# Pairs and layer-1 blocks two to a PSUM bank, one stage order for another, and the first ids spread by TensorE

## The chip, the cores and the metric

The kernel runs on one core of a Trainium2 chip. The metric is the device time of one execution in microseconds (us). The engines are TensorE (PE in the rows; PEld is its weight load), VectorE (DVE), ScalarE (ACT), GpSimd (POOL) and SyncE (SP), which here only issues DMAs.

## The reference: what is computed

A recommender tower for 2048 samples. Per sample 26 ids pick one row of 128 floats from each of 26 tables; with the dense row these are 27 features. All pairwise dot products go with the dense row into three layers.

```python
e = jnp.stack([tbl_0[ids[:, 0]], ..., tbl_25[ids[:, 25]]], axis=1)       # 2048 x 26 x 128
combined = jnp.concatenate([dense[:, None, :], e], axis=1)               # 27 features
inter = jnp.einsum('bfd,bgd->bfg', combined, combined)[:, TRIU_I, TRIU_J]  # 351 pairs
h = jnp.concatenate([dense, inter, dense], axis=1)
h = jnp.maximum(h @ W_top1 + b_top1, 0.0)        # 607 -> 512
h = jnp.maximum(h @ W_top2 + b_top2, 0.0)        # 512 -> 256
y = h @ W_top3                                   # 256 -> 1
```

## The kernel before

The batch is cut into 8 steps of 256 samples (`NB`, `BS`), two tiles of 128 each. The rows of a sample come in two ways.

- Ten small tables (1000 rows) are held in SBUF as two parts, `table_hi` and `table_lo`. A **lookup** is a multiplication by a one-hot matrix: ACT writes the spread ids into PSUM (`idb`, L555), DVE compares them with the row numbers in two chunks (L651, three slots `SLOTS`), PE multiplies 16 times (L411, L412). In step 0 four of the tables are taken from the raw table instead (L409). The ids arrive spread over 128 partitions by one DMA for each lookup (L275), the first ten of them into free places of `rows`.
- The other 16 tables are **gathered** from HBM by indirect DMAs of GpSimd (L359), 128 rows each, in groups of eight. After the first five, group g waits until products stage g-4 is done (`wait_for_turn`), so each products stage lets one burst of eight gathers go. PE transposes what landed (`rows`, L431), ACT or DVE copies it into `XT` (L567, L666).

The **products** of a step are four stages of 64 small products (L449: one record for each half, 128 records), copied by ACT and DVE in turn (L573, L659). **Unblock** (L461, copies L578 and L674) and **pairs** (L472, copies L584) bring the products into the layout that **layer1** (L483, L485; four blocks), **layer2** (L494; two blocks) and **layer3** (L503) take; their results leave by ACT (L588, L595).

The order of all this is one list written out by hand, `stages()`, and PE, ACT, DVE and SP each walk through it and do their part. Layers run one step behind the products, lookups one step ahead. All stages but the products share a ring of four PSUM banks in the order of the list: before PE fills a bank it waits until the bank's last user but three has been copied out (`claim`). So whoever waits for a copy, waits for everything that stands before it on ACT or DVE.

In what follows a step has four **quarters**, each from the end of one products stage to the end of the next; the first begins behind products 0.

## Time and profile before

| | us |
|---|---|
| median of 3 runs (lowest, highest) | 520.28 (514.35, 523.56) |
| the profiled execution | 515.3 |
| its span, first to last instruction | 513.2 |
| granted TensorE clock, mean | 0.88 |
| busy: PE, DVE, POOL, ACT | 408.8, 262.7, 254.1, 208.7 |
| chain that ended last: PE, issue, ACT, SPq, DMA | 71%, 13%, 4%, 4%, 4% |

All positions in time are those of the profiled execution, whose own time lies 2.1 us over its span. A granted clock of 1.00 is 2.4 GHz and one of 0.50 is 1.2 GHz; values between are means over a stretch.

### The profile page before, as it was taken

The numbers are of one execution on the slowest core, as the hardware profiler recorded it, in microseconds if no ns is written. First come the engines' busy times: TensorE is split into PE (matmuls) and PEld (weight loads), VectorE is DVE, ScalarE is ACT, GpSimd is POOL, SyncE is SP. The second block draws the span as 40 slices with busy tenths as digits, with TensorE's granted clock in tenths as the row PEclk, the third lists the DMA queues.
The fourth block names the chain that finished last, engine by engine and source line by source line (L and its number), as shares of the span: only waits on it lengthen the run. The fifth ranks groups of instructions, "written<-read, shape, count | busy, mean of one in ns | idle before, by whom it ended". The sixth has DMA issues, their size and how long they took to land.

```text
span 513.2 us, 14192 instructions
## 1 busy us (share of the span) xinstructions
PE 408.8 (80%) x6280; PEld 365.9 (71%) x6280; DVE 262.7 (51%) x323; ACT 208.7 (41%) x436; POOL 254.1 (50%) x265
## 2 busy tenths in 40 slices
PE   5886727777978598875978788887989689789977
PEld 4776716767878497764967687785878588778755
DVE  3789505654555554663553655655364655454220
ACT  3456302234343543444342553435243543337432
POOL 5778875551555555552555535553555535540000
PEclk8998857776999898988897978997898969899989
DMA  6994251230322222221222212221232212210000
GB/s 170 227 240 107 67 158 50 70 108 23 74 59 78 56 64 68 69 64 32 64 66 70 63 49 64 67 74 49 68 68 69 63 42 70 58 39 1 4 1 0
DMA packets 27972, 36.34 MB, mean 71 GB/s; under 512 B 9151, under 2 KB 21959, under 8 KB 27912
## 3 DMA queue, kind: packets, MB, share of 16 engines
q1 hardware_dynamic: 19704, 18.65, 14.6%
q0 software_dynamic: 8192, 16.79, 13.5%
q8 instruction: 49, 0.80, 0.6%
q14 instruction: 11, 0.09, 0.0%
q10 hardware_dynamic: 16, 0.01, 0.0%
HBM read 35.42 MB, written 0.01 MB: 69 GB/s over the span
## 4 chain that ended last, share of the span: by engine, by line
PE 71%; issue 13%; ACT 4%; SPq 4%; DMA 4%; DVE 2%; another core or an unknown queue 1%; ACTq 0%; DVEq 0%
PE ring L411 17%; PE ring L412 15%; PE gram L449 10%; PE ring L485 8%; PE ring L431 7%; PE ring L494 6%; DMA dense<-in_r_dense_features 4%; PE ring L483 3%; SPq L281 2%; PE ring L461 2%; PE ring L472 2%; DVE pairs_and_more L674 2%; PE ring L503 2%; ACT pairs_and_more L578 1%; SPq L275 1%
## 5 line engine op out<-in xcount | busy, mean ns | idle before, releaser
L359 POOL DMA_INDIRECT rows<-in_tbl,ids_all x256 | 248.7, 971 | 201.1 <-PE gram L449 127.3
L651 DVE TENSOR_TENSOR onehot<-idb,vrow 125x1024 fp32r<-125x1024 f32 x160 | 192.7, 1222 | 130.5 <-PE ring L412 58.7
L411 PE MATMUL ring<-onehot,table_hi 125*128 125x256 f32 x608 | 181.6, 328 | 22.1 <-DVE pairs_and_more L674 7.6
L412 PE MATMUL ring<-onehot,table_lo 125*128 125x256 f32 x608 | 169.5, 309 | 0.0
L411 PEld LDWEIGHTS ring<-onehot,table_hi 125*128 125x128 f32 x608 | 132.9, 219 | 28.8 <-issue 8.7
L412 PEld LDWEIGHTS ring<-onehot,table_lo 125*128 125x128 f32 x608 | 133.4, 219 | 0.8
L559 ACT COPY xt<-ring 128x256 f32<-128x256 f32 x80 | 54.2, 677 | 128.9 <-PE ring L412 68.3
L449 PE MATMUL gram<-xt 128*27 128x26 f32 x4096 | 55.1, 201 | 42.6 <-issue 40.0
L449 PEld LDWEIGHTS gram<-xt 128*27 128x27 f32 x4096 | 47.8, 114 | 51.7 <-issue 46.0
L567 ACT COPY xt<-ring 128x512 f32<-128x512 f32 (+1 forms) x56 | 51.2, 987 | 24.1 <-remote 16.0
L431 PE MATMUL ring<-ident,rows 128*128 128x128 f32 x256 | 38.6, 285 | 13.6 <-issue 6.7
L485 PE MATMUL ring<-x,w 128*128 128x256 f32 (+1 forms) x192 | 47.7, 385 | 0.0
L666 DVE COPY xt<-ring 128x512 f32<-128x512 f32 x24 | 28.4, 1183 | 31.5 <-PE ring L431 19.7
L431 PEld LDWEIGHTS ring<-ident,rows 128*128 128x128 f32 x256 | 30.8, 147 | 18.2 <-issue 10.0
L485 PEld LDWEIGHTS ring<-x,w 128*128 128x128 f32 (+1 forms) x192 | 37.5, 195 | 5.6
L588 ACT ACTIVATE h<-ring,b 128x256 f32<-128x256 f32 x32 | 15.2, 475 | 55.8 <-PE ring L485 17.8
L659 DVE COPY A<-gram 128x416 f32<-128x416 f32 x16 | 14.2, 886 | 42.3 <-PE gram L449 42.3
L674 DVE COPY pairs_and_more<-ring 64x80 f32<-64x80 f32 (+6 forms) x112 | 22.1, 197 | 22.3 <-PE ring L431 12.6
L494 PE MATMUL ring<-h,w 128*128 128x256 f32 x128 | 31.5, 391 | 1.0 <-ACT h L588 1.0
L555 ACT CAST idb<-ids_spread 128x256 f32<-128x256 int32 x70 | 30.6, 437 | 3.6 <-ACT pairs_and_more L595 2.0
L494 PEld LDWEIGHTS ring<-h,w 128*128 128x128 f32 x128 | 24.0, 196 | 4.7 <-ACT h L588 1.8
L578 ACT COPY pairs_and_more<-ring 64x104 f32<-64x104 f32 (+5 forms) x96 | 21.2, 221 | 10.7 <-PE ring L431 9.4
(41 smaller groups left out, 209.7 us busy)
## 6 DMA issues: line engine op xcount, KB each, us to landing
ids_spread<-in_ids_t SPq DMA_DIRECT2D x70, 128.0 KB
rows<-in_tbl,ids_all POOLq DMA_INDIRECT x256
xt<-in_tbl SPq DMA_DIRECT2D x6, 448.0 KB
w<-in_tbl SPq DMA_DIRECT2D x3, 448.0 KB
rows<-in_ids_t SPq DMA_DIRECT2D x10, 128.0 KB, 5.7
dense<-in_r_dense_features SPq DMA_DIRECT2D x16, 64.0 KB
w<-in_W_top SPq DMA_DIRECT2D x4, 256.0 KB
w<-in_W_top SPq DMA_DIRECT2D x1, 512.0 KB
```

Of the source, the lines that this page charges most:

```text
L359: pool.indirect_dma_start(rows[:, i % ROWS, :], None, aps[f"tbl_{f}"], bass.IndirectOffsetOnAxis(ap=ids_all[:, k, f:f + 1].bitcast(U32), a ...
L411: pe.matmul(ps, table_hi[:, m, c * KC + k, :], chosen, start=first, stop=False)
L412: last = pe.matmul(ps, table_lo[:, m, c * KC + k, :], chosen, start=False, stop=final)
L431: last = pe.transpose(ps[:, i * P:(i + 1) * P], src, ident[:])
L449: last = pe.matmul(gram[QW * j:QW * j + F, s % 2, g * NA:(g + 1) * NA], sample, sample[:, 0:NA], start=True, stop=True)
L485: last = pe.matmul(ps, w1[0:w, 1 + k, b * P:(b + 1) * P], x[0:w, k, :], start=False, stop=(k == KX - 1))
L494: last = pe.matmul(ps[:, 0:BS], w2[:, k, b * P:(b + 1) * P], h1[:, k, :], start=(k == 0), stop=(k == H1 // P - 1))
L555: act.copy(idb[:, u % 2, 0:BS], ids_place(u)).then_inc(idb_ready, 1)
L559: act.copy(XT[:, n % 2, :, 1 + NG + m], ps[:, 0:BS]).then_inc(left("lookup", n, m, 0), 1)
L567: act.copy(rows_view(n, t, g), ps[:, 0:f * P].rearrange("d (f s) -> d f s", f=f)).then_inc(left("rows", n, t, g), 1)
L651: dve.tensor_tensor(onehot[:, (CH * u + c) % SLOTS], idb[0:VP, u % 2, 0:BS].unsqueeze(1).to_broadcast([VP, KC, BS]), vrow[:, c * KC:(c + 1 ...
L674: last = dve.tensor_copy(dst, src)
```

## The change

- The pairs take two ring banks instead of three, layer1 two instead of four: two blocks of 256 columns lie side by side in a bank. ACT copies the first two pair blocks with one instruction, and still does one activation for each layer-1 block, but PE is told of the bank only after both.
- `stages()` is another list: in a steady step some other work stands between any two lookups; pairs go from the end of a step to the first quarter of the next; layer1 is two stages instead of four; rows 0 and 1 of the next step move from the last quarter to the third; layer3 moves to the end of the last quarter.
- ACT now copies all of tile 0's rows and products 1 and 3; DVE copies rows 1 and 3 of tile 1 and products 0 and 2.
- The ids of the first ten lookups come as one small DMA of ten rows. ACT turns them into floats, and PE spreads each over the partitions with one multiplication (`spread_first_ids`); the ten broadcast DMAs, and GpSimd's waits for their places, are gone. `ids_all`, which the gathers need, is issued after that small DMA. The dense tiles are loaded between the tables instead of after them.
- DVE makes the first chunk of a lookup one stage earlier, and `lower_part` before the chunks.

```diff
-        yield from lookups(0, *range(NL - 2))
-        yield from rows(0, 0, 0, 1)
-        yield from lookups(0, NL - 2)
-        yield from rows(0, 0, 2, 3, 4)
+        yield "first_ids", 0, 0, 0
+        yield "first_ids", 0, 1, 0
+        for m in range(NL - 1):
+            yield from lookups(0, m)
+            if m + 2 < NL:
+                yield "first_ids", 0, m + 2, 0
+        yield from rows(0, 0, 0, 1, 2, 3, 4)
         yield from lookups(0, NL - 1)
         for n in range(NB):
+            first, last = n == 0, n == NB - 1
             yield "products", n, 0, 0
             yield from lookups(n + 1, 0)
+            yield from layer("pairs", n - 1, 0, 1)
+            yield from lookups(n + 1, 1)
             yield from layer("layer1", n - 1, 0)
-            yield from lookups(n + 1, 1)
-            yield from layer("layer1", n - 1, 1)
+
+            yield "products", n, 1, 0
             yield from lookups(n + 1, 2)
-
-            yield "products", n, 1, 0
-            if n == 0:
+            if first:
                 yield from lookups(n + 1, 3)
             yield from rows(n, 1, 0, 1)
-            yield from layer("layer1", n - 1, 2)
-            if n > 0:
+            yield from layer("layer1", n - 1, 1)
+            yield from rows(n, 1, 2, 3, 4)
+            if not first:
                 yield from lookups(n + 1, 3)
-            yield from rows(n, 1, 2, 3)
-            yield from layer("layer1", n - 1, 3)
-            yield from rows(n, 1, 4)
+            if last:
+                yield from layer("layer2", n - 1, 0)
+
+            yield "products", n, 2, 0
             yield from lookups(n + 1, 4)
-            if n == NB - 1:
+            if not last:
                 yield from layer("layer2", n - 1, 0)
-
-            yield "products", n, 2, 0
             yield from lookups(n + 1, 5)
-            if n < NB - 1:
-                yield from layer("layer2", n - 1, 0)
+            yield from rows(n + 1, 0, 0, 1)
+            if not last:
+                yield from layer("layer2", n - 1, 1)
             yield from lookups(n + 1, 6)
-            yield from layer("layer2", n - 1, 1)
+
+            yield "products", n, 3, 0
+            if last:
+                yield from layer("layer2", n - 1, 1)
             yield from lookups(n + 1, 7)
-            if n < NB - 1:
-                yield from layer("layer3", n - 1, 0)
-
-            yield "products", n, 3, 0
-            if n == NB - 1:
-                yield from layer("layer3", n - 1, 0)
+            yield from layer("unblock", n, 0, 1)
             yield from lookups(n + 1, 8)
-            yield from layer("unblock", n, 0, 1)
-            yield from rows(n + 1, 0, 0, 1)
             yield from layer("unblock", n, 2, 3)
             yield from rows(n + 1, 0, 2, 3, 4)
             yield from lookups(n + 1, 9)
-            yield from layer("pairs", n, 0, 1, 2)
-        yield from layer("layer1", NB - 1, 0, 1, 2, 3)
+            yield from layer("layer3", n - 1, 0)
+        yield from layer("pairs", NB - 1, 0, 1)
+        yield from layer("layer1", NB - 1, 0, 1)
...
+            sp.dma_start(first_ids_i, aps["ids_t"][:, 0:BS]).then_inc(first_ids_landed, 16)
             sp.dma_start(ids_all[:], ids.rearrange("(t p) f -> p t f", p=P)).then_inc(ids_landed, 16)
             for m in range(NL):
-                spread_ids(m)
                 load_raw(m)
-            load_dense(0)
-            load_dense(1)
+                if m in (3, 6):
+                    load_dense(m // 4)
...
+            def spread_first_ids(m):
+                if m == 0:
+                    pe.wait_ge(first_ids_ready, 1)
+                if m >= 2:
+                    pe.wait_ge(onehot_ready, CH * (m - 1))
+                pe.matmul(idb[0:VP, m % 2, 0:BS], ident[0:NL, m:m + 1].to_broadcast([NL, VP]), first_ids, start=True,
+                          stop=True).then_inc(first_idb_ready, 1)
...
+                bank = claim("layer1", n, b, 0)
+                for i in range(2):
+                    ps, block = bank[:, i * BS:(i + 1) * BS], slice((2 * b + i) * P, (2 * b + i + 1) * P)
+                    pe.matmul(ps, w1[:, 0, block], x_dense[:, n % 2, :], start=True, stop=False)
+                    if b == i == 0:
+                        wait_emptied("pairs", n, 1, 0)
```

On PE, the second quarter of a steady step, behind its first lookup; the names are those of the stages above (`dense` and `rows` are row transposes, `x_dense` and `x` layer1). Before, it begins with products 1:

```order
L449 MATMUL gram<-xt 27x26 x64
L431 MATMUL ring<-ident,dense 128x128
L431 MATMUL ring<-ident,rows 128x128 x7
L483 MATMUL ring<-x_dense,w 128x256
L485 MATMUL ring<-x,w 128x256 x3
L411 MATMUL ring<-onehot,table_hi 128x256
L412 MATMUL ring<-onehot,table_lo 128x256
```

After the change, from the last multiplication of that quarter's first lookup to the first of its second:

```order
L418 MATMUL ring<-onehot,table_lo 128x256
L437 MATMUL ring<-ident,dense 128x128
L437 MATMUL ring<-ident,rows 128x128 x7
L490 MATMUL ring<-x_dense,w 128x256
L495 MATMUL ring<-x,w 128x256 x3
L490 MATMUL ring<-x_dense,w 128x256
L495 MATMUL ring<-x,w 128x256 x3
L437 MATMUL ring<-ident,rows 128x128 x9
L417 MATMUL ring<-onehot,table_hi 128x256
```

Two layer-1 blocks and all the remaining row transposes now stand in one piece ahead of the lookup, where one block stood before.

On PE, the last quarter of a steady step, before: both halves of unblock (`A`), with rows 0 and 1 of the next step between them.

```order
L461 MATMUL ring<-ident,A 128x128 x6
L431 MATMUL ring<-ident,dense 128x128
L431 MATMUL ring<-ident,rows 128x128 x7
L461 MATMUL ring<-ident,A 128x128 x7
L431 MATMUL ring<-ident,rows 128x128 x9
L411 MATMUL ring<-onehot,table_hi 128x256
```

After the change, the same place from the last multiplication of the lookup that now stands between the halves:

```order
L418 MATMUL ring<-onehot,table_lo 128x256
L467 MATMUL ring<-ident,A 128x128 x7
L437 MATMUL ring<-ident,rows 128x128 x9
L417 MATMUL ring<-onehot,table_hi 128x256
```

A lookup has taken the place of rows 0 and 1; what stands behind it, the second half of unblock, nine transposes and a lookup, is unchanged.

On ACT, the end of that quarter after the change, from the row copies to the next step's first pairs:

```order
L574 COPY xt<-ring 128x4x128 x2
L574 COPY xt<-ring 128x128
L562 CAST idb<-ids_spread 128x256
L566 COPY xt<-ring 128x256
L610 COPY pairs_and_more<-ring 1x4x64
L615 DMA out_y<-pairs_and_more 1x256
L562 CAST idb<-ids_spread 128x256
L566 COPY xt<-ring 128x256
L591 COPY x<-ring 128x512
L591 COPY x<-ring 95x256
```

Before, three copies L584 of the pairs stand directly behind the first L559 there, and the output copy two lookups further up.

## Rows read from the trace of the kernel before

**Rows 1.** Windows: us; busy PE, PEld, DVE, ACT, POOL; clock; DMA share; GB/s.

```profile
303.20:316.30 13.10, 11.58 (x194) 10.59 (x193) 6.03 (x5) 4.74 (x9) 7.56 (x8) 0.96 0.28 70
316.30:330.20 13.90, 12.02 (x195) 11.01 (x194) 7.94 (x8) 5.57 (x10) 7.57 (x8) 0.92 0.25 57
330.20:343.10 12.90, 11.53 (x197) 10.43 (x197) 6.83 (x6) 5.10 (x10) 7.57 (x8) 1.00 0.29 79
343.10:360.50 17.40, 13.50 (x203) 11.81 (x203) 10.66 (x22) 9.32 (x25) 7.56 (x8) 0.78 0.22 54
460.40:471.80 11.40, 10.27 (x203) 9.21 (x203) 6.78 (x18) 8.22 (x22) 0.00 (x0) 1.00 0.02 4
...
126.40:446.30 319.90, 264.87 (x4301) 241.21 (x4301) 172.81 (x208) 133.50 (x285) 166.47 (x176) 0.90 0.26 63
...
387.50:401.80 14.30, 12.89 (x198) 11.79 (x199) 6.43 (x7) 5.37 (x11) 7.56 (x8) 0.90 0.29 71
105.90:126.20 20.30, 15.43 (x204) 13.92 (x203) 10.78 (x21) 9.01 (x23) 7.56 (x8) 0.67 0.16 44
```

**Rows 2.** Timeline, POOL: start, us, instruction, idle before, its releaser.

```profile
303.49 0.95 POOL L359 DMA_INDIRECT rows<-in_tbl,ids_all  x1 [7.11 <-PE gram L449]
...
312.26 0.94 POOL L359 DMA_INDIRECT rows<-in_tbl,ids_all  x1 [0.30 <-issue]
```

**Rows 3.** Timeline, PE: the products stage behind the burst of rows 2.

```profile
312.54 0.37 PE L449 MATMUL gram<-xt 128*27 128x26 f32 x14
...
314.84 1.49 PE L449 MATMUL gram<-xt 128*27 128x26 f32 x111 [0.54 <-issue]
```

**Rows 4.** Timeline, PE and ACT: layer2's second block and its activation.

```profile
335.77 1.89 PE L494 MATMUL ring<-h,w 128*128 128x256 f32 x8
...
340.42 0.47 ACT L588 ACTIVATE x<-ring,b 128x256 f32<-128x256 f32 x1 [2.89 <-PE ring L412]
```

**Rows 5.** Timeline, all engines: the last quarter of step 4.

```profile
343.02 0.38 PE L411 MATMUL ring<-onehot,table_hi 125*128 125x256 f32 x1
...
343.38 0.94 POOL L359 DMA_INDIRECT rows<-in_tbl,ids_all  x1 [3.21 <-PE gram L449]
...
345.04 0.82 PE L461 MATMUL ring<-ident,A 128*128 128x128 f32 x6
...
347.28 1.02 PE L461 MATMUL ring<-ident,A 128*128 128x128 f32 x7 [0.29 <-issue]
...
351.88 1.49 DVE L674 COPY pairs_and_more<-ring 64x32 f32<-64x32 f32 x8 [2.38 <-remote]
353.43 0.58 PE L411 MATMUL ring<-onehot,table_hi 125*128 125x256 f32 x1 [1.35 <-issue]
354.75 2.45 ACT L567 COPY xt<-ring 128x512 f32<-128x512 f32 x3 [3.06 <-remote]
...
357.14 1.75 PE L472 MATMUL ring<-ident,pairs_and_more 64*128 64x64 f32 x12
```

**Rows 6.** Timeline, POOL and PE: gathers behind the start, and products 1.

```profile
50.90 4.71 POOL L335 TENSOR_TENSOR table_lo<-w,table_hi 125x1024 fp32r<-125x1024 f32 x2
55.77 0.97 POOL L359 DMA_INDIRECT rows<-in_tbl,ids_all  x1 [0.16 <-PE ring L412]
...
60.49 0.54 PE L449 MATMUL gram<-xt 128*27 128x26 f32 x40
...
79.03 0.81 PE L449 MATMUL gram<-xt 128*27 128x26 f32 x47 [1.89 <-issue]
```

**Rows 7.** Groups of instructions: busy us, mean ns of one, idle before.

```profile
L567 ACT COPY xt<-ring 128x512 f32<-128x512 f32 x40 | 45.9, 1202 | 23.3 <-remote 16.0 <-PE ring L431 4.6 <-PE ring L485 2.0
...
L588 ACT ACTIVATE h<-ring,b 128x256 f32<-128x256 f32 x32 | 15.2, 475 | 55.8 <-PE ring L485 17.8 <-PE ring L412 16.5 <-remote 14.0
```

**Rows 8.** Timeline, PE: unblock and pairs at the end of the program.

```profile
491.19 1.61 PE L461 MATMUL ring<-ident,A 128*128 128x128 f32 x13
...
495.12 1.02 PE L472 MATMUL ring<-ident,pairs_and_more 64*128 64x64 f32 x12 [2.33 <-DVE pairs_and_more L674]
```

More of the change, by code:

```diff
@@ L148, in rows_on_vector @@
     def rows_on_vector(t, g):
-        return g == 1 or (t, g) == (1, 3)
+        return t == 1 and g in (1, 3)
     def unblock_on_vector(b):
@@ L510, in _ @@
             for stage, n, a, b in stages():
-                if stage == "lookup":
+                if stage == "first_ids":
+                    spread_first_ids(a)
+                elif stage == "lookup":
                     lookup(n, a)
@@ L579, in store_unblocked, with store_pairs, store_layer1, store_layer2 @@
                 last.then_inc(left("unblock", n, b, 0), 1)
-            def store_pairs(n, k):
-                w = K_PAIR[k][1]
-                ps = bank("pairs", n, k, 0)
-                act.copy(x[0:w, k, :], ps[0:w, 0:BS]).then_inc(left("pairs", n, k, 0), 1)
-            def store_layer(stage, n, b, h_next, bias):
-                ps = bank(stage, n, b, 0)
-                act.activation(h_next[:, b, :], ps[:, 0:BS], ACT.Relu, bias=bias[:, b:b + 1]).then_inc(left(stage, n, b, 0), 1)
+            def store_pairs(n, b):
+                ps = bank("pairs", n, b, 0)
+                k, w = (slice(0, 2), P) if b == 0 else (slice(2, 3), K_PAIR[2][1])
+                act.copy(x[0:w, k, :].rearrange("p k s -> p (k s)"), ps[0:w, 0:(k.stop - k.start) * BS]).then_inc(
+                    left("pairs", n, b, 0), 1)
+            def store_layer1(n, b):
+                ps = bank("layer1", n, b, 0)
+                for i in range(2):
+                    block = 2 * b + i
+                    last = act.activation(h1[:, block, :], ps[:, i * BS:(i + 1) * BS], ACT.Relu, bias=b1[:, block:block + 1])
+                last.then_inc(left("layer1", n, b, 0), 1)
+            def store_layer2(n, b):
+                ps = bank("layer2", n, b, 0)
+                act.activation(h2[:, b, :], ps[:, 0:BS], ACT.Relu, bias=b2[:, b:b + 1]).then_inc(left("layer2", n, b, 0), 1)
             def store_y(n):
@@ L616, in _ @@
                     store_rows(n, a, b)
-                elif stage == "products" and a % 2 == 0:
+                elif stage == "products" and a % 2 == 1:
                     store_products(n, a)
@@ L699, in _ @@
                     store_unblocked(n, a)
-                elif stage == "products" and a % 2 == 1:
+                elif stage == "products" and a % 2 == 0:
                     store_products(n, a)
```

98 lines of the change are left out of this document (44 added, 54 removed).

## The prediction

> **What bounds the kernel now.** I read the chain that ended last first: PE holds 71% of it, ACT 4%, DVE 2%. That says PE-bound, yet PE is busy 80% of the span, so I cut the steady part into quarters. From 126.4 to 446.3 there are 22 bursts of eight gathers (176 instructions on POOL), so a quarter takes 319.9 / 22 = 14.5 us [rows 1]. In step 4 the quarters take 13.1, 13.9, 12.9 and 17.4 us. The one in row 460.40 holds the same kind of work as the 17.4 us one, but no gathers (POOL busy 0.00), and takes 11.4 us [rows 1]. So gathers cost time on engines that don't run them.
>
> Where is seen against the start of a burst (I write +x for x us after its first gather). A burst issues eight gathers from 303.49 to 313.2 [rows 2]. In its second half the signals of PE reach the others late: the last matmul of layer2's second block begins about 337.3 and ends at 337.7, ACT is idle and starts on it at 340.42, or +9.9 [rows 4]. In the last quarter unblock's second half is issued by 348.3 (+4.9); DVE begins at 351.88 (+8.5), and ACT takes up three row copies at 354.75 (+11.4) after 3.06 us of idling [rows 5]. The products stage itself, 128 tiny records, gets 14 through at 312.54 and the last 111 only from 314.84, +11.4 [rows 3]. Behind the start 16 gathers run in one piece from 55.77: products 1 begins at 60.49 and gets its last 47 through at 79.03, +23.3 [rows 6]. Both fit 1.43 to 1.45 us for each gather. The cause inside the chip no row shows; I take the pattern: reports of PE are prompt to about +5, late between, and all there at +11.4.
>
> Two rules follow. A products stage reached before +11.4 still ends about 1.25 us later, and the next burst starts then, so **a quarter with a burst cannot be under 12.9 us**. Quarters over that are lengthened by something that PE waits for. That is what the change can win.
>
> **The change, quarter by quarter of a steady step.** Durations: a lookup 2.0 us (343.02 to 345.04), a transpose 0.13 (six in 0.82) [rows 5], a row copy 1.2 and a layer activation 0.48 on ACT [rows 7], eight halves of a layer product 1.89 [rows 4], so a pair of layer-1 blocks 3.6. Each quarter begins at -0.3.
>
> *First quarter*: products 0 lies before it; lookup, pairs 1.5, lookup, layer-1 pair: products 1 is reached near +9, held to +11.4, ends at +12.7. It was 13.1, at its floor; pairs are hidden in the hold. Gain 0.
>
> *Second*: lookup to 1.8, rows 0 and 1 to 2.8, the layer-1 pair to 6.3, rows 2 to 4 to 7.3. The next lookup claims layer1's bank. Its report falls in the late stretch, +8.5 as for unblock; ACT then needs two activations, 0.95, so the lookup runs +9.5 to +11.5. Products 2 waits for row copy 3 on DVE, reported at +11.4, and for row copies 2 and 4 on ACT: start +12.6 to +13.0, end near +14. The quarter took 13.9; I keep 14.0. Were all reports one gather earlier it would be 13.4; one later, 15. The Trainium skill ("Perfetto Trace Analysis", Optimizing Scalar/DVE Operations) speaks against the merged bank: where ScalarE isn't saturated but causes bubbles elsewhere, breaking instructions up lets work complete sooner. The trace agrees in kind, ACT is busy 5.57 of 13.9 us there [rows 1], and by that rule one bank for each block would give these 0.48 us back; the bank's second activation is in the 9.5 above.
>
> *Third*: it took 12.9 in step 4 and 14.3 in row 387.50, since layer3 stood before products 3 and waited for layer2's late activation, at +9.9 or +11.4 [rows 1, 4]. Now only lookups and two row transposes follow layer2, and no copy of them is needed; PE has 2.0 + 1.9 + 2.0 + 1.0 + 1.9 + 2.0 = 10.8 us to do and is held to +11.4. I expect 12.9 each time. With two thirds of these quarters near 14.2, that gains **0.9**.
>
> *Last*: what set it is a chain: unblock's fourth part reported at +8.5, DVE copy 1.49, the last lookup at 353.43 (+10.1) at half clock, 3.8 us, pairs at 357.14, products 0 at 358.8 [rows 5]. Beside it ACT has three row copies from +11.4, 2.45 us, an id copy, and the lookup's copy. Nothing here is removed but pairs (12 transposes, 1.75), and layer3 (4 halves, 0.9 to 1.7) stands there instead. Rows 0 and 1 leave, 0.95 of PE, but a lookup comes before unblock's second half and it is issued at +5.2 instead of +4.9: same report. So the largest quarter is hardly touched. I take **0.7** (17.6 to 16.9); bounds 0, and 2.0 if the row copies are reported a gather sooner.
>
> Sum for a steady step: 1.6 us; steps 1 to 5: **8.0**, and step 6, whose last quarter has no gathers, **1.4**.
>
> **The start.** Ten broadcast DMAs of 128 KB go, tables land sooner and the lookups of step 0 with them. But the start is paced by GpSimd: 32 gathers to 50.9, then `lower_part` 4.71, then 16 more from 55.77, which hold products 1 [rows 6]. They are not removed, and their first waits 0.4 longer for `ids_all`. What changes is products 1: two lookups after products 0 instead of three, it can start about 57 (+2) and pass before the hold, not at 79. Then group 6 queues right behind, 24 gathers in one piece hold products 2 until 55.4 + 34.3, end 91, where before it ended at 92.9 (79.8 + 13.1). Products 3 follows at +12.9: **2.0** to 3.5 gained; I take 2.6. If products 1 is caught, 0.5. The last quarter of step 0 took 20.3 at clock 0.67 [rows 1], with half-rate lookups; I take 0.9 off for the same reasons as above.
>
> **The end.** Step 7 has no gathers. Pairs of step 6 now stand in it: 1.04, and 0.3 of wait for their copy, as layer1 follows at once: 1.3 lost. At the other end, unblock (491.19 to 492.8) was followed by a 2.33 us wait for its copies [rows 8]; now layer2 and unblock come ahead of layer3, which fills it: 2.4 gained, and 0.5 where layer2 waited for four blocks' reports less the merged activation. Net **1.6** gained.
>
> Sum: 8.0 + 1.4 + 2.6 + 0.9 + 1.6 = 14.5 us, so 515.3 - 14.5 = 500.8, or 0.972. On the median of 520.28, which lies 5 us above the profiled execution, that is **505.6 us**.
>
> **The rivals.** *Only start and end move* (the quarters are set by late reports, so the change doesn't do in them what it says): the third quarter's gain is eaten by the second, which loses the 1.1 us of a report one gather later. Left are 2.6 + 0.9 + 1.6 = 5.1: 515. For it: the chain of the last quarter stays as it was. Against: layer3's wait does go.
>
> *The floor everywhere*: moving the row copies and layer reports out of the late stretch brings second and last quarters to 13.4 and 15.3: 2.2 us more in six steps, 27 us in all: 493. For it: fewer bank reports, 31 for 34 in a step. Against: those in the last quarter's late stretch are the same ones.
>
> *Slower*: half clock at the start of the second and last quarters. Products 1 is now reached near +9 and idles until +11.4 each time, and row 105.90 shows what a last quarter costs that starts at 1.2 GHz: 20.3 instead of 17.4 [rows 1], because with the lookup in front of it unblock's second half is issued at +8 and reported at +11.4, not +8.5. In the second quarter the layer-1 pair at half rate takes 7 us and is reported at +11.4: 2 us more. Price 4.9 us in each of 7 steps, 34 in all: 535 on the profiled execution, 540 on the median. It decides from three steps on. Against it: products 1 idled as long before (312.9 to 314.8 [rows 3]) with clock 0.92 behind it. The Trainium skill ("TensorE: Matmul & The Clock Gate", HAM oscillation) describes this: gaps between bursts let the gate fall back and each next burst starts cold. By that rule alone this is the outcome; the clock of 0.96 to 1.00 in step 4's first three quarters bears it out only in part.
>
> **Chances.** Forecast 0.50, only start and end 0.22, floor 0.15, slower 0.08; 0.05 for what I haven't seen. The range 493 to 517 leaves out the slower case and the outer half of the floor, and takes in the bounds of the second quarter (-0.6 to +1.0 in each step) and the last (0 to 2.0). About 2% is what a measurement of this kernel can tell from no change, here 10.4 us, and my likeliest gain is not far over it: faster 0.60, same 0.32, slower 0.08.
>
> **What would show it.** In the profile after: last instructions 13 to 16 us earlier; third quarters all at 12.9; first quarters at 12.9 with products 1 held; a last quarter near 17, with three row copies of ACT beginning at +10 to +11.4; products 1 of step 0 done by 60; no wait of 2 us before the last pairs. I am wrong if a quarter with a burst is much under 12.9 (then the hold isn't the gathers' doing), if layer1's bank is the wait of the second quarter beyond +9.5, or if the clock at the start of last quarters is 0.50.

## The result and the profile after

The changed kernel takes **526.67 us** (median of 4 runs, 526.03 to 529.53), the kernel before 519.9 (4 runs): ratio 1.0203, 95% interval 1.0142 to 1.0264. It is slower, and whether by more or less than 2% the interval leaves open; 505.6 was forecast and the range ended at 517. In a later job of its own (e5) the ratio was 1.0228 (1.0094 to 1.0362). Ratios here and below leave out the runs that lie over 1.5% above the fastest of the same kernel, medians do not, so the two can differ.

The windows of the trace after that answer to those of [rows 1]: the four quarters of step 4, the last quarter of step 6 (no gathers), all 22 quarters with a burst, the last quarter of step 0. Columns as there.

```profile
312.00:325.10 13.10, 10.93 (x191) 9.76 (x189) 5.72 (x5) 3.62 (x8) 7.55 (x8) 0.93 0.24 63
325.10:338.00 12.90, 11.78 (x198) 10.82 (x195) 5.68 (x5) 6.44 (x11) 7.54 (x8) 0.94 0.22 59
338.00:351.00 13.00, 11.81 (x201) 10.88 (x201) 7.78 (x8) 5.18 (x10) 7.55 (x8) 1.00 0.31 77
351.00:370.00 19.00, 13.25 (x203) 11.52 (x203) 11.17 (x22) 10.18 (x27) 7.55 (x8) 0.82 0.26 57
470.60:482.40 11.80, 10.80 (x203) 9.62 (x204) 7.35 (x19) 8.67 (x22) 0.00 (x0) 1.00 0.01 3
133.30:457.60 324.30, 264.28 (x4304) 236.88 (x4297) 163.53 (x201) 135.73 (x284) 166.05 (x176) 0.90 0.25 61
113.90:133.30 19.40, 12.99 (x200) 11.88 (x199) 10.87 (x21) 8.83 (x23) 7.56 (x8) 0.76 0.30 82
```

The reader is to see that PE's work in the 22 quarters is the same (264.3 us, before 264.9) and their length is not: 324.3 for 319.9. The quarter that grew is the last one, 19.0 for 17.4. Cut at the ends of the products stages, the two traces differ like this (means of steps 1 to 5, us; the last column is a second trace of the changed kernel, e5):

| | before | forecast | after | e5 |
|---|---|---|---|---|
| products 3 of step 0 end at | 105.9 | 103.3 | 113.9 | 112.8 |
| first quarter | 13.0 | 12.9 | 13.0 | 12.9 |
| second | 14.3 | 14.0 | 13.7 | 14.3 |
| third | 13.7 | 12.9 | 13.3 | 13.0 |
| last | 17.6 | 16.9 | 19.5 | 19.5 |
| last of step 0 | 20.3 | 19.4 | 19.5 | 19.2 |
| end of products 0 of step 7 to the end | 41.4 | 39.8 | 42.4 | 42.2 |

The medians are 6.8 us apart, the two traces 11.6, since the traced run of before was one of its faster ones. Of the 11.6 us between the two spans (524.8 and 513.2) 8.0 arise in the start and 4.1 in steps 1 to 5, where the last quarters lose 9.3 and the others give 5.2 back; step 0's last quarter and step 6 give 1.5 back, and the end loses 1.0. A second trace of before (e6, below) has last quarters of 18.4, so the two traces of each kernel put their loss at 1.1 to 1.9 us each.

**The last quarter.** Timeline of step 5's, after, with the burst's first gather at 410.85:

```profile
410.85 0.94 POOL L355 DMA_INDIRECT rows<-in_tbl,ids_all  x1 [3.61 <-PE gram L455]
...
412.51 0.82 PE L467 MATMUL ring<-ident,A 128*128 128x128 f32 x6
...
415.08 0.93 PE L467 MATMUL ring<-ident,A 128*128 128x128 f32 x7
...
415.85 0.60 PE L437 MATMUL ring<-ident,rows 128*128 128x128 f32 x4
...
419.30 0.66 ACT L566 COPY xt<-ring 128x256 f32<-128x256 f32 x1 [4.33 <-remote]
...
420.01 1.23 ACT L585 COPY pairs_and_more<-ring 64x56 f32<-64x56 f32 x6
420.02 1.12 PE L437 MATMUL ring<-ident,rows 128*128 128x128 f32 x4 [3.57 <-ACT xt L566]
...
422.18 1.49 DVE L690 COPY pairs_and_more<-ring 64x32 f32<-64x32 f32 x8 [1.58 <-PE ring L437]
422.23 2.43 ACT L574 COPY xt<-ring 128x512 f32<-128x512 f32 x3 [1.00 <-PE ring L437]
423.72 0.58 PE L417 MATMUL ring<-onehot,table_hi 125*128 125x256 f32 x1 [1.95 <-DVE pairs_and_more L690]
```

Lookup 8 ends at 415.08, where unblock's second half begins (+4.2); ACT idles for 4.33 us and starts on its copy at +8.45. PE waits 3.57 us for that copy, because the row transposes need its bank. Unblock's second half is issued by +5.2, as the prediction had it, but DVE gets it at +11.3, not at +8.5 as before [rows 5]: a report now stands ahead of it. How much later it comes does not follow from that alone: one report more, at one each 1.43 us, would have made it +9.9. The last lookup starts at +12.9 instead of +10.1, at half clock as before. The half clock comes behind the wait and not before it: four transposes take 0.60 us at 415.85 and 1.12 us at 420.02, when PE has stood for 3.57 us.

**The start.** Timeline of step 0, after: PE spreads an id (L397), DVE and PE go on with the lookups, while 16 gathers run in one piece from 4.91 to 25.2.

```profile
19.60 0.69 PE L397 MATMUL idb<-pairs_and_more,ident 10*125 10x256 f32 x2
...
22.02 1.23 DVE L667 TENSOR_TENSOR onehot<-idb,vrow 125x1024 fp32r<-125x1024 f32 x1 [4.41 <-remote]
...
24.43 0.58 PE L417 MATMUL ring<-onehot,table_hi 125*128 125x256 f32 x1 [4.15 <-issue]
...
27.79 0.66 ACT L566 COPY xt<-ring 128x256 f32<-128x256 f32 x1 [6.39 <-remote]
...
31.40 0.94 POOL L355 DMA_INDIRECT rows<-in_tbl,ids_all  x1 [6.20 <-PE ring L418]
...
57.35 1.27 PE L455 MATMUL gram<-xt 128*27 128x26 f32 x128 [1.03 <-ACT xt L566]
```

DVE idles for 4.41 us, PE for 4.15, ACT for 6.39, and GpSimd, which waits for lookup 3, for 6.20. Products 0 begin at 57.35, before at 50.5. Nothing of it is made up: products 1 begin at 64.00, are caught by the next 16 gathers and end at 85.2.

**The end.** PE in step 7:

```profile
495.88 1.91 PE L455 MATMUL gram<-xt 128*27 128x26 f32 x202
500.06 0.64 PE L455 MATMUL gram<-xt 128*27 128x26 f32 x54 [2.27 <-issue]
500.63 3.67 PE L504 MATMUL ring<-h,w 128*128 128x256 f32 x8
```

Products 2 and 3 stand back to back there, 256 small records in one piece. After 202 of them PE stands still for 2.27 us with nothing that it waits for, and layer2's block behind it runs at half clock (3.67 for 1.99). The half clock does not belong to the standstill: in e16, below, the same block takes 1.99 us behind the same stop, and before has a stretch at half clock of its own there (496.1 to 499.6).

```profile
488.18 0.64 PE L455 MATMUL gram<-xt 128*27 128x26 f32 x54 [2.30 <-issue]
488.75 1.99 PE L504 MATMUL ring<-h,w 128*128 128x256 f32 x8
```

### The profile page after: what moved, and what is told of

It is laid out like the page before. It is cut to its first block, busy times and chain, and to the rows that moved or that the text cites. A ratio compares the mean times of both kernels' runs of the same rounds, so it can differ in the third digit from the quotient of the medians.

```text
span 524.8 us, 14191 instructions
## 1 busy us (share of the span) xinstructions
PE 411.1 (78%) x6300; PEld 360.4 (69%) x6300; DVE 253.3 (48%) x315; ACT 209.5 (40%) x427; POOL 250.5 (48%) x265
## 3 DMA queue, kind: packets, MB, share of 16 engines
q1 hardware_dynamic: 18284, 17.35, 13.5%
q0 software_dynamic: 8192, 16.79, 12.7%
## 4 chain that ended last, share of the span: by engine, by line
PE 64%; issue 11%; another core or an unknown queue 10%; ACT 7%; DVE 7%; POOL 0%; DVEq 0%; POOLq 0%
PE ring L417 14%; PE ring L418 13%; PE gram L455 9%; PE ring L495 7%; PE ring L504 6%; PE ring L437 5%; PE ring L415 3%; DVE onehot L667 3%; PE ring L490 2%; DVE xt L682 2%; ACT xt L566 2%; ACT pairs_and_more L585 2%; PE ring L513 2%; DVE pairs_and_more L690 2%
## 5 line engine op out<-in xcount | busy, mean ns | idle before, releaser
L355 POOL DMA_INDIRECT rows<-in_tbl,ids_all x256 | 245.0, 957 | 216.2 <-PE gram L455 134.0
L417 PE MATMUL ring<-onehot,table_hi 125*128 125x256 f32 x608 | 175.8, 321 | 19.5 <-issue 6.7
L418 PE MATMUL ring<-onehot,table_lo 125*128 125x256 f32 x608 | 165.7, 304 | 1.2 <-issue 1.2
L417 PEld LDWEIGHTS ring<-onehot,table_hi 125*128 125x128 f32 x608 | 130.4, 215 | 28.1 <-issue 9.1
L418 PEld LDWEIGHTS ring<-onehot,table_lo 125*128 125x128 f32 x608 | 130.8, 215 | 1.5 <-issue 1.4
L437 PE MATMUL ring<-ident,rows 128*128 128x128 f32 x256 | 39.9, 292 | 35.5 <-ACT xt L566 24.6
L574 ACT COPY xt<-ring 128x512 f32<-128x512 f32 (+1 forms) x64 | 59.6, 1022 | 14.1 <-remote 6.7
L682 DVE COPY xt<-ring 128x512 f32<-128x512 f32 x16 | 18.5, 1169 | 45.0 <-remote 25.3
L598 ACT ACTIVATE h<-ring,b 128x256 f32<-128x256 f32 x32 | 13.4, 470 | 46.4 <-PE ring L495 17.1
L690 DVE COPY pairs_and_more<-ring 64x80 f32<-64x80 f32 (+6 forms) x112 | 22.0, 196 | 15.6 <-PE ring L437 7.2
L580 ACT COPY A<-gram 128x416 f32<-128x416 f32 x16 | 14.9, 934 | 28.5 <-PE gram L455 28.5
```

Source lines behind the costliest of these rows:

```text
L355: pool.indirect_dma_start(rows[:, i % ROWS, :], None, aps[f"tbl_{f}"], bass.IndirectOffsetOnAxis(ap=ids_all[:, k, f:f + 1].bitcast(U32), a ...
L417: pe.matmul(ps, table_hi[:, m, c * KC + k, :], chosen, start=first, stop=False)
L418: last = pe.matmul(ps, table_lo[:, m, c * KC + k, :], chosen, start=False, stop=final)
L437: last = pe.transpose(ps[:, i * P:(i + 1) * P], src, ident[:])
L574: act.copy(rows_view(n, t, g), ps[:, 0:f * P].rearrange("d (f s) -> d f s", f=f)).then_inc(left("rows", n, t, g), 1)
L690: last = dve.tensor_copy(dst, src)
```

## The experiments

Sixteen runs in five jobs; e5 and e6 are the two kernels once more, e10, e11 and e16 repeat e4, e3 and e2. In the first job (e1 to e4) something was different: the kernel before took **404.04 us** (13 runs), in all other jobs 518 to 522. In the traces of that job no report of PE is held behind gathers; in all the others they are. The same program (e2 and e16) takes 402.3 and 513.1. The expectations speak of two kinds of chip; that does not hold, as the record has one chip number, 13, for the first job and for that of e8 to e11, where reports are held. I call the two conditions *prompt* and *held*; comparisons are made within a job or a condition. Most rows of the table are one trace each. Quarters are means of steps 1 to 5, from the ends of the products stages; "start" is the end of step 0's products 3.

| run | order, edit | condition | start | quarters | span |
|---|---|---|---|---|---|
| e6 | before | held | 110.5 | 13.0 13.8 14.2 18.4 | 515.9 |
| e5 | changed | held | 112.8 | 12.9 14.3 13.0 19.5 | 524.4 |
| e1 | changed, old ids | prompt | 78.6 | 10.4 11.0 11.7 14.3 | 419.2 |
| e2 | changed, lookup 8 behind unblock | prompt | 75.5 | 10.5 11.1 11.8 12.1 | 399.6 |
| e16 | as e2 | held | 108.3 | 13.0 13.9 13.0 18.6 | 511.2 |
| e7 | both of e1 and e2 | held | 108.7 | 12.9 13.9 13.5 18.6 | 515.0 |
| e9 | changed, before's last quarter | held | 112.1 | 13.0 13.8 15.6 17.2 | 523.9 |
| e3 | changed, loads for gathers | prompt | 74.5 | 9.9 10.8 11.5 13.7 | 403.9 |
| e11 | as e3 | held | 97.5 | 9.9 10.8 11.5 13.6 | 425.8 |
| e8 | changed, bursts cut in two | held | 114.5 | 13.0 14.3 13.0 15.1 | 508.5 |
| e4 | changed, 0.42 us between gathers | prompt | 76.0 | 10.3 10.9 11.9 14.7 | 426.4 |
| e10 | as e4 | held | 111.7 | 13.1 13.4 13.3 14.3 | 491.2 |
| e14 | as e10, from the first gather on | held | 99.9 | 13.5 13.3 13.3 14.1 | 487.1 |
| e12 | before, 0.42 us between gathers | held | 109.3 | 13.2 13.3 13.3 13.4 | 480.4 |
| e13 | changed, three edits | held | 111.6 | 12.8 12.8 12.9 14.0 | 480.5 |
| e15 | before, 0.30 us between gathers | held | 110.3 | 12.8 12.9 12.9 13.3 | 474.2 |

**e1, the first ids as before.** The spreads by PE out, the ten broadcast DMAs and ACT's casts in:

```diff
-        yield "first_ids", 0, 0, 0
-        yield "first_ids", 0, 1, 0
-        for m in range(NL - 1):
-            yield from lookups(0, m)
-            if m + 2 < NL:
-                yield "first_ids", 0, m + 2, 0
+        yield from lookups(0, *range(NL - 1))
```

> The changed kernel with the first ids as before: ten broadcast DMAs into places of rows, ACT casts them, the dense tiles behind the tables. All else stays changed. Theory: in the changed kernel products 0 of step 0 began 6.9 us later because each spread by PE has to be reported to DVE, and from 5 us on these reports are held by 16 gathers in one piece, so that ACT's casts must bring products 0 back to about 51 (from 57.35) and the end of step 0's products 3 to near 107 (from 113.9): 7 us off, 519 to 521 on the median. Rival: the order of the stages in step 0 (all rows behind nine lookups, DVE's chunks one stage earlier) makes the start late: then the time stays at 525 to 528.

Measured, with prompt reports: 417.7 us, 1.0338 (1.0267 to 1.041) of before. The expectation was for held reports, so it can't be judged here; but with prompt ones the new ids look like the better start (74.5 to 76.0 in e2, e3 and e4, 78.6 here). The trace is that of the slowest of the four runs (414.0 to 421.1).

**e2 and e16, lookup 8 behind unblock's second half**, in either condition:

```diff
-            yield from lookups(n + 1, 8)
             yield from layer("unblock", n, 2, 3)
+            yield from lookups(n + 1, 8)
```

> The changed kernel with lookup 8 of the last quarter moved behind unblock's second half. Theory: a report of PE that is sent later than about 4 us after a burst's first gather waits in a row, one for each gather; lookup 8 between the halves made unblock's second half the next in that row (reported at +11.3 where before had +8.5). With the lookup behind it both halves end before +4 and are reported at once; the last quarter takes 15 to 16.5 us instead of 19.5 (five steps), 505 to 511 on the median. Rival: half clock, not the order of reports, makes the last quarter 19.5 long: then it stays over 18.5 and the time within 3 us of 526.7.

> e2 once more, for a chip on which reports are held. As in e7, both halves of unblock are reported at once, but the last lookup then waits for lookup 8's bank, which is reported only at the end of the burst: last quarters of 18.2 to 18.9 instead of 19.5, the start as in the changed kernel, 519 to 525. If they come to 17 or less, e7's 18.6 was the start's doing. Where nothing is held: 400 to 405 again.

With prompt reports the last quarter falls from e1's 14.3 to 12.1, and the kernel is level with before: 0.9965 (0.993 to 1.0001). The windows of step 4's last quarter, e1 and then e2:

```profile
269.70:284.10 14.40, 12.26 (x203) 10.48 (x203) 10.00 (x21) 9.27 (x24) 7.57 (x8) 0.88 0.26 69
```

```profile
259.00:270.60 11.60, 10.83 (x203) 9.60 (x203) 9.93 (x21) 9.42 (x24) 7.57 (x8) 1.00 0.39 80
```

So the lookup between the halves costs about 2 us a quarter and clock even where nothing is held (the first ids, in which e1 and e2 differ too, touch step 0 alone); e4, which also has it there, shows 14.7, and e3, without gathers, 13.7. With held reports taking it out gains only 0.9 (19.5 to 18.6). That is in the range given for e16, but far from the 15 to 16.5 of e2's theory, and over the 18.5 that e2's text named as the mark of its rival, the half clock. So half clock is part of what makes the held last quarter long: PE is busy for 12.7 us of e16's last quarter in step 3, at a granted clock of 0.82, and for 10.8 us at 1.00 in e2's in step 4. e16 took 513.05 us, 6 less than expected, mainly as its start ended at 108.3.

**e5, e6, e7** in one job, held:

> The changed kernel, unchanged, beside runs of before on the same chip. The four runs before this one fell on a chip where before takes 404 us and not 520; in their traces no report of PE is held behind the gathers, and the last quarters take 14.3 with lookup 8 between the halves of unblock (old start) and 12.1 with it behind. If this falls on such a chip: the start of e2 (75.5 at the end of step 0's products 3) and the last quarters of e1 give 399.6 + 5 x 2.2 + 2 = 413 to 416, 3% over before. If it falls on one like the first: 524 to 530.

> The kernel before, once more, for its trace on the same chip as the others of this call. If no report is held there: quarters of 10 to 12.5 us, mean clock over 0.97, 401 to 406 us. If they are held: 12.9, 14, 13.7, 17.6 as in the first trace, and 514 to 524.

> The changed kernel with the first ids as before and with lookup 8 behind unblock's second half. On a chip without held reports: e2's quarters with e1's start, 3 us later at the end of step 0's products 3, 403 to 406. On one with held reports: the last quarters 3 to 4 shorter than 19.5, and the start back at 107 from 113.9: 499 to 506, 3 to 4% under before. Rival: the start is not the spreads' doing; then 506 to 512 there.

e5 repeats the result. e6 shows how much two traces of the kernel before differ: 110.5 for 105.9 at the start, 18.4 for 17.6 in the last quarters. e7 came to 517.11 us, 1.0106 (1.001 to 1.0202), 11 us over the range I gave and 5 over its rival's. Timeline of its last quarter in step 3, first gather at 285.50:

```profile
287.16 1.60 PE L470 MATMUL ring<-ident,A 128*128 128x128 f32 x13
...
287.81 2.79 ACT L589 COPY pairs_and_more<-ring 64x104 f32<-64x104 f32 x12
...
291.42 1.15 PE L440 MATMUL ring<-ident,rows 128*128 128x128 f32 x9
...
296.90 0.67 ACT L570 COPY xt<-ring 128x256 f32<-128x256 f32 x1 [6.03 <-remote]
...
297.61 0.58 PE L420 MATMUL ring<-onehot,table_hi 125*128 125x256 f32 x1 [5.05 <-ACT xt L570]
```

Unblock is copied at once, as foreseen. But now lookup 8, ended at 291.4 (+5.9), is the one held, to +11.4, and the last lookup waits 5.05 us for its bank. A held stretch is not got rid of by reordering; the wait goes to the next stage that needs a bank.

**e9, before's last quarter.**

```diff
-            yield from rows(n + 1, 0, 0, 1)
...
-            yield from lookups(n + 1, 6)
+            yield from lookups(n + 1, 6, 7)
...
-            yield from lookups(n + 1, 7)
+            yield from lookups(n + 1, 8)
             yield from layer("unblock", n, 0, 1)
-            yield from lookups(n + 1, 8)
+            yield from rows(n + 1, 0, 0, 1)
```

> The changed kernel with the last quarter's order of before: lookup 7 back in the third quarter, lookup 8 ahead of unblock, rows 0 and 1 between its halves (pairs stay in the next step's first quarter, layer3 at the end). Theory: lookup 8 between the halves costs the last quarter 1.9 us in each of five steps; here they take 17 to 17.7 instead of 19.5, third quarters 13 to 14.3: 516 to 521 where reports are held. Rival: pairs and layer3's move lengthen the last quarter, not lookup 8: then 19 or more, 525 to 528. Where nothing is held: last quarters 12.5 to 13 for 14.3, 406 to 409.

The last quarter comes to 17.2, as expected, with pairs and layer3 where the change put them: neither of those moves is its trouble. But the edit does more than undo the placement of lookup 8: it takes lookup 7 out of the last quarter, which then has two lookups instead of three, and the third quarter has four (before has three) and goes from 13.0 to 15.6. So of the 2.3 us that the last quarter falls the placement alone isn't shown to have more than e16's 0.9, and the whole gains nothing: 531.04 us, 1.0236 (1.0136 to 1.0336) of before, 10 over the range given. The last and the third quarter of step 3:

```profile
291.70:308.00 16.30, 12.16 (x199) 9.89 (x195) 8.44 (x19) 10.74 (x25) 7.54 (x8) 0.90 0.21 57
276.20:291.70 15.50, 12.80 (x210) 12.00 (x209) 9.84 (x10) 4.60 (x10) 7.55 (x8) 1.00 0.27 71
```

**e3 and e11, plain loads by SP in place of the gathers** of groups 5 and up (rows then don't belong to the ids).

```diff
+            def direct_group(group):
+                sp.wait_ge(gram_ready, group - 4)
...
+                    sp.dma_start(rows[:, i % ROWS, :], aps[f"tbl_{GATHER_TABLES[g]}"][0:P, :]).then_inc(
+                        direct_landed[k % 3][g // GROUP], 16)
```

> The changed kernel, with the gathers of groups 5 and up left out: in their place SP loads the first 128 rows of each table, the same 64 KB for each, at the same turns (rows are then not those of the ids). Theory: the gathers on GpSimd hold the reports of PE; without them no quarter is held, first and third quarters fall from 12.9 to 11 to 11.8 us, last ones from 19.5 to about 12, as in step 6's last quarter (11.9), and the whole to 455 to 470. Rival: the row traffic itself or PE's own work sets 12.9: then first and third quarters stay at 12.5 or more and the whole over 500.

> e3 once more (from group 5 on plain loads by SP in place of the gathers), for a chip on which reports are held. If the gathers hold them: quarters of e3, 9.9, 10.8, 11.5 and 13.7 behind step 0, the whole 435 to 450 (step 0 keeps its gathers). If the chip's DMA or its row traffic is slower in general: first quarters stay over 12, over 500. On a chip without held reports again 404 to 407.

Windows of e11, held: a first quarter (step 4), all from the end of step 0 to the end of step 6's products 3, and a last quarter.

```profile
248.80:258.60 9.80, 9.80 (x189) 8.86 (x189) 5.63 (x5) 3.62 (x8) 0.00 (x0) 1.00 0.31 84
97.50:372.50 275.00, 261.13 (x4696) 238.98 (x4695) 180.99 (x228) 148.09 (x317) 0.00 (x0) 0.98 0.33 81
280.90:293.90 13.00, 11.08 (x203) 9.67 (x204) 9.91 (x21) 9.38 (x24) 0.00 (x0) 1.00 0.33 74
```

427.6 us beside before's 518.4, and 7 under the range given for it. Behind step 0 the two runs of this kernel are alike to 1.1 us (329.4 and 328.3), and the 23 us between them lie in step 0, which keeps its gathers. So the two conditions differ only while gathers run: the hold is theirs. Both runs are far under e3's 455 to 470, since I had taken 11 to 11.8 for a quarter without gathers and not 9.9 to 11.5.

**e8, each burst cut in two.**

```diff
+                    if g % GROUP == GROUP // 2 and i // GROUP >= 5 + STEPS:
...
+                        pool.wait_ge(ring_filled, filled(*half, 0))
```

> The changed kernel with each group of eight gathers from step 1's first on cut in two: four at once, and the other four only when a stage near the middle of the quarter is filled (lookup 1, layer-1 pair 1, layer2 block 0, unblock's last part). Theory (where reports are held): only what is sent with over some four gathers behind it is held, so two bursts of four have no or short holds, quarters fall to 11.5 to 12.5 and last ones to 14 to 16: 480 to 500. Rival: the hold lasts 1.43 us a gather whatever the grouping, the second four hold from the middle of the quarter to its end: 530 to 550. Where nothing is held: within 3 us of the changed kernel there, 413.

510.77 us, before 518.4; the theory had said 480 to 500, its rival 530 to 550, so neither holds. Last quarters 15.1 for 19.5, but the others stay at 13 to 14.3, outside the theory's 11.5 to 12.5. In a first quarter the cut hardly cuts, the fifth gather goes at +5.9 instead of +5.0, so the run tells little of those.

**e4 and e10, gathers spaced**: one subtraction on GpSimd behind each gather but a group's last.

```diff
+                    if i >= 5 * GROUP and g % GROUP < GROUP - 1:
+                        u = (i // GROUP - 5) * (GROUP - 1) + g % GROUP
+                        if u:
+                            pool.wait_ge(paused, u)
+                        pool.tensor_tensor(idle, ident[:], ident[:], ALU.subtract).then_inc(paused, 1)
```

> The changed kernel with one small subtraction (128x128) on GpSimd after each gather of groups 5 and up but a group's last, so that gathers are issued about 1.6 us apart instead of 1.25, and 44 places for rows instead of 45. Theory A, the held reports come from a backlog (issued each 1.25, done each 1.43): at 1.6 apart none builds up, quarters fall to 11.5 to 12.5 where the burst of 12 to 13 us allows it, the whole to 480 to 500. Theory B, each gather holds the reports whatever the distance: bursts now last 12.8 us and the hold ends with them, quarters of 14 to 14.5 instead of 12.9, the whole 545 to 560.

> e4 once more (a small subtraction on GpSimd after each gather), for a chip on which reports are held. There: backlog, 480 to 500; a hold for each gather whatever the distance, 545 to 560. On a chip without held reports again 426 to 431, since GpSimd's longer bursts then set the pace of the rows.

Held: 493.01 us beside before's 518.4. Timeline of e10, POOL: a gather each 1.55 us.

```profile
223.41 0.97 POOL L356 DMA_INDIRECT rows<-in_tbl,ids_all  x1 [0.16 <-issue]
224.40 0.41 POOL L364 TENSOR_TENSOR idle<-ident 128x128 f32<-128x128 f32 x1
224.97 0.96 POOL L356 DMA_INDIRECT rows<-in_tbl,ids_all  x1 [0.16 <-issue]
```

More work on GpSimd, and the last quarters fall by 5.2 us. Theory A (a backlog: each issued after 1.25, done after 1.43) foretold the sign and the whole; theory B is out. Its quarters of 11.5 to 12.5 didn't come, though: they don't go under 13.1, as a products stage is still slowed until the burst, now longer, has ended. With prompt reports the pause is a loss (e4, 428.24 us beside before's 404.04): GpSimd falls behind, and step 7's second quarter, in which PE waits 6.92 us for the last rows, takes 18.0 us instead of e1's 10.5.

**e14, the first 40 gathers spaced too.**

> e10 with the first 40 gathers spaced as well. Where reports are held: if held reports of the spreads and chunks make the start late, products 0 of step 0 begin at 47 to 52 instead of 57.4, and step 0's products 3 end 3 to 7 us before 111.7: 486 to 490. Rival: tables or the longer run of gathers set the start: products 0 at 57 or later, 493 to 500. Where nothing is held: products 0 at 47 to 48 as in e2.

Timeline of e14, PE, products 0 of step 0, first and last lines:

```profile
44.12 0.93 PE L463 MATMUL gram<-xt 128*27 128x26 f32 x48 [1.07 <-ACT xt L574]
45.51 0.41 PE L463 MATMUL gram<-xt 128*27 128x26 f32 x20 [0.46 <-issue]
46.38 0.27 PE L463 MATMUL gram<-xt 128*27 128x26 f32 x6 [0.46 <-issue]
...
53.03 0.34 PE L463 MATMUL gram<-xt 128*27 128x26 f32 x8 [0.41 <-issue]
```

Products 0 begin at 44.1, 13 us sooner than in e10, with the same spreads and tables: held reports made the start late. Both moved further than expected (47 to 52, and an end of the start 3 to 7 us sooner): the start ends 11.8 us sooner, but 7.8 of it are lost in step 0's last quarter, 23.5 for 15.7; 488.95 us.

**e12, e13, e15.** e12 puts e4's edit on the kernel before, e15 shortens its pause to 128x64 (0.30 us). e13 is the changed kernel with that pause, e2's edit and this one:

```diff
-            if last:
-                yield from layer("layer2", n - 1, 0)
-
             yield "products", n, 2, 0
             yield from lookups(n + 1, 4)
-            if not last:
-                yield from layer("layer2", n - 1, 0)
+            yield from layer("layer2", n - 1, 0)
```

> The kernel before with the small subtraction (128x128, 0.42 us) on GpSimd after each gather of groups 5 and up but a group's last, and 44 places for rows, as in e10. Where reports are held: if the changed order is worse only because of held reports, it gains as much here and the last quarter comes to 14 to 15, the whole to 484 to 494, level with e10's 493 or under it by the start's 3 to 5 us. Rival: the changed order is the better one once reports are prompt, then this stays over 497. Where nothing is held: 418 to 430, for the pace of GpSimd.

> The changed kernel with three edits: a shorter pause (128x64) after the same gathers, lookup 8 behind unblock's second half, and layer2's first block of the last step behind products 2 as before, so that no two products stages stand back to back. Where reports are held: a gather each 1.45 us or so, quarters of 12.3 to 12.9, last ones 13 to 14, no gap in products 3 of step 7 (2.3 us in every run of the changed order so far): 470 to 482, 8% under before. Rival: at 1.45 apart the backlog is back, quarters 12.9 and last ones over 16: over 492. Where nothing is held: 405 to 415.

> e12 with the pause cut from 0.42 to 0.30 us (128x64 instead of 128x128), so that gathers are issued 1.44 us apart instead of 1.55. Where reports are held: quarters of 12.8 instead of 13.3, as in e13, 22 of them, 10 us less than e12: 470 to 478, 8 to 9% under before. Rival: 1.44 is too near to the 1.43 that a gather takes, reports are held again in the last quarters of before's order: over 483. Where nothing is held: 412 to 422.

Measured: e12 483.86 us, 0.9261 (0.9102 to 0.942) of before, its last quarters at 13.4 under the 14 to 15 expected; e13, in the same job, 482.29, at the edge of its range; **e15 476.52 us, 0.9102 (0.8998 to 0.9206)**, the lowest median of all while reports are held, and faster than both kernels. A last quarter each of e12, e13 (step 3) and e15 (step 4):

```profile
268.70:282.00 13.30, 10.96 (x204) 9.59 (x203) 10.35 (x21) 8.40 (x23) 10.59 (x15) 1.00 0.25 67
```

```profile
270.90:284.80 13.90, 11.06 (x203) 9.62 (x203) 9.83 (x20) 9.64 (x24) 9.84 (x15) 1.00 0.25 67
```

```profile
318.90:331.90 13.00, 10.66 (x205) 9.45 (x203) 10.45 (x21) 8.72 (x23) 9.80 (x15) 1.00 0.24 67
```

With the same pause the old order has the shorter last quarters, 13.4 against e10's 14.3, 13.3 against e13's 14.0, in one trace each and of different jobs. Of the whole times only e10's is apart (493.0 beside e12's 479.2 to 486.4); e13's four runs (475.1 to 484.3) and e15's (471.8 to 482.5) overlap, so which order is better with the short pause is not settled. In e13 the stop in the last products stage has shrunk to 0.23 us:

```profile
456.38 0.82 PE L458 MATMUL gram<-xt 128*27 128x26 f32 x74
457.44 0.65 PE L458 MATMUL gram<-xt 128*27 128x26 f32 x54 [0.23 <-issue]
458.01 1.99 PE L507 MATMUL ring<-h,w 128*128 128x256 f32 x8
```

## Why the prediction was wrong

The forecast of 500.8 us for the profiled execution was 25.8 us short of the measured 526.6. The start (10.6), five last quarters (13.0) and the end (2.6) make that up.

- **What bounds the kernel: right.** That gathers hold PE's reports was the base of the forecast. e11 shows it: the same quarters without gathers take 9.9, 10.8, 11.5 and 13.6. The floor of 12.9 held to 0.2 us in every quarter with a burst of the held traces with gathers at 1.25 us.
- **First quarter: right**, 13.0, pairs hidden in the hold. **Second: right**, 13.7 and 14.3 beside 14.0 forecast, and products 2 of step 5 began at +12.6, as written; but layer1's bank was taken up at +7.1 (390.48), not at +8.5, so that bank was not what the end waited for. **Third: right**, 13.3 and 13.0 beside 12.9, with one of 14.3 left in the first trace; over five steps it gave the one gain that both traces have, 1.9 us (3.5 in e5).
- **Last quarter: the step that failed.** "A lookup comes before unblock's second half and it is issued at +5.2 instead of +4.9: same report" is wrong in its last two words. It was issued at +5.2 and reported at +11.3, as lookup 8's report, sent at +4.2 and delivered at +8.45, stood ahead of it. I had looked at when the half is issued and not at its place among the reports. Forecast 0.7 gained, measured 1.9 lost (1.1 against e6), 13 us under the forecast over five steps. Undoing this placement alone gives 0.9 back with held reports (e16) and about 2.2 with prompt ones (e1 and e2); what e9 gives beyond that comes with a lookup less in the quarter.
- **The start: wrong.** Two steps failed: "the start is paced by GpSimd", and that its gathers are not touched. They wait for lookups 3 and 6, and those became slow; each spread is one more report of PE under a burst. Products 1 was to pass "before the hold" at 57 and began at 64.0. Forecast 2.6 gained, measured 8.0 lost. Of these some are chance: the first ids of before ended the start at 105.9 to 110.5 (e6, e7, e12, e15 and the first trace, mean 108.9), those of the change at 108.3 to 114.5 (seven, without e11 and e14, mean 112.1), so the change's own part is about 3, no more than the spread within either group (4.6 and 6.2). Products 0 themselves begin at 50.2 to 57.7 with the new ids and at 50.5 to 57.2 with the old ones. e14 shows that held reports make the start late. That the spreads add to it is argued, and not shown: the one run with the order of the change and the old ids under held reports is e7, and its start ends at 108.7.
- **The end: wrong** by 2.6. The gap before the last pairs is filled for the most part, two waits of 0.58 and 0.73 us for one of 2.33. But "layer2 and unblock come ahead of layer3" put products 2 and 3 back to back: 2.27 us of standstill and 1.7 at half clock. I had costed what stands ahead of a wait, and not that it had kept the products stages apart. What that is worth is less than its 2.27 us: with layer2's block back between them (e13) the third and fourth quarter of step 7 take 11.6 us instead of 12.2, as products 2 then wait 1.30 us for a row copy. The half clock comes and goes between traces with the same stages there: the end takes 40.7 to 40.8 in e2, e7 and e16, which all have the standstill and no half clock, beside 40.0 in e6 without it, and 42.4 and 42.2 beside 41.4 with it.
- **The rivals.** None of their times came; 526.7 lies between only start and end (515) and slower (540). Part of the slower case's mechanism did: I had written that unblock's second half would be reported at +11.4, not +8.5, with the lookup in front, but made it depend on half clock at the quarter's start. All ten last quarters of the two traces of the change start at a granted clock of 1.00. With 8% I had it far too low, since my own words for it held without the clock. The rule of the Trainium skill in "TensorE: Matmul & The Clock Gate" (HAM oscillation) is borne out in kind, within the quarters: in step 5's last quarter PE stands for 3.57 us and comes back at half clock. But before has that too: the mean granted clock of the last quarters is 0.80 before and 0.77 after.

What stays open is how a gather on GpSimd holds a report of PE, and why one job of five was free of it. It isn't the landing of the rows: by the packets in the traces, those of a gather in the steady part have mostly landed 2.1 to 3.3 us after its start in e2 and in e16 alike. The Trainium skill says in "Perfetto Trace Analysis" (DMA Instruction — SWDGE (GPSIMD)) that a profile's end of a GpSimd DMA is the end of writing its descriptors, not of the data's movement. The trace agrees, with 0.95 us for the instruction and 2.1 to 3.3 for the rows; but it doesn't explain reports that are late until +11.4, about when the rows of the last gather, started at +8.8, land. Whether the new order gains with prompt reports was not measured for the changed kernel itself, only for e1 (3.4% slower) and e2 (level).

## What to carry to other kernels

Where one engine's reports are late behind a burst on another, moving stages only moves the wait: count the reports in the late stretch and in which place each stands, not only when it is issued. Better still, thin out the burst: a pause of 0.3 us behind seven of eight gathers was worth 9%, four times what the order of the stages cost. That holds while reports are held; in the job without held reports a pause of 0.42 us cost 6% (e4, 428.2 beside 404.0). And measure the kernel before in every job: here it took 404 us in one and 518 to 522 in the others.

## What the runs showed that I had not expected

- The same program takes 402.3 and 513.1 us (e2, e16), with the same instructions and transfers; the difference lies wholly where gathers run on GpSimd.
- Bursts of eight gathers issued 1.25 us apart hold reports of PE for up to 5.5 us (e7: lookup 8 ended at 291.4, its copy began at 296.90). Of the semaphore updates by PE that the traces record, 84 (before) and 85 (after) come over 1 us behind the end of the multiplication that sent them; with gathers 1.55 apart 6 and 7 do (e10, e12), 1.44 apart 15 and 30 (e13, e15), and 2 in e2. But a stage of 128 small multiplications is still let through in pieces of 4 to 10 records, one each 0.73 us, with gathers 1.55 apart (e14).
- In the 256 small multiplications in one piece PE stands still for 2.0 to 2.3 us, in both conditions and without any gather running, in all thirteen traces that have them. The place is fixed in PE's list of instructions: behind its multiplication 6157 in eleven of the traces, and 6158 in e1 and e7, which have no spreads, so that this is 21 small ones further on in the stage. The stop of 0.23 us in e13, with only 74 small ones directly ahead of it, stands behind 6157 too. A 16 KB instruction load (queue q8) begins within 0.41 us of each of the long stops. That points to the loading of instructions; no run tried it.
